# Residual block with per-image mixed 3x3 kernels: two whole-image passes move to GpSimd, conv1 groups are evacuated whole, and the prologue and the order of steps are rewritten

## What is computed

```python
xn = (x - mean_c) / sqrt(var_c + 1e-5)                    # per image and channel
gate = softmax(mean_pixels(xn) @ gate_w.T + gate_b)       # 7 experts
kw1 = sum_e gate[e] * experts_w1[e] + conv1_w             # 32x32x3x3, likewise kb1, kw2, kb2
out1 = relu(conv3x3(xn, kw1) + kb1)
out  = x + (xn + conv3x3(out1, kw2) + kb2)
```

## Time and profile before

| what | value |
|---|---|
| time, median of 3 runs | 386.82 us |
| the 3 runs | 386.42, 389.31, 386.82 us |
| span of the profiled execution | 389.2 us |
| time nearest to that span | 389.31 us |
| mean granted TensorE clock | 0.940 of full speed |
| busy PE, DVE, ACT, POOL | 326.8, 308.1, 300.3, 44.5 us |
| DMA, share of 16 engines' span | 69.7% |

### The profile page before, as it was taken

One profiled execution on the slowest core, in us unless ns is written; L12 is line 12 of the kernel. 1 busy time (PEld: TensorE's weight loads), 2 busy tenths in 40 slices (PEclk: granted clock), 3 DMA queues, 4 the chain that ended last, 5 costly groups with the idle time before them and its releaser, 6 DMA issues.

```text
span 389.2 us, 8418 instructions
## 1 busy us (share of the span) xinstructions
PE 326.8 (84%) x2983; PEld 198.4 (51%) x2983; DVE 308.1 (79%) x709; ACT 300.3 (77%) x373; POOL 44.5 (11%) x80
## 2 busy tenths in 40 slices
PE   3218698996999699996979979996999979999984
PEld 2117345654555355653535555653656545655663
DVE  4899978988689886998688797898689897777432
ACT  2357499986897968977897868978789768976950
POOL 7262302010100101010000101010010101000000
PEclk9556999998999989998999989999999989999998
DMA  7949915495948959396856949497885956092354
GB/s 169 224 95 196 205 30 125 107 203 137 202 92 187 182 142 220 86 210 148 178 127 149 223 111 203 96 196 147 188 167 123 217 128 147 22 207 53 92 123 121
DMA packets 107146, 58.19 MB, mean 149 GB/s; under 512 B 102496, under 2 KB 103008, under 8 KB 107104
## 3 DMA queue, kind: packets, MB, share of 16 engines
q1 hardware_dynamic: 106912, 57.62, 69.7%
q0 software_dynamic: 192, 0.01, 0.1%
HBM read 19.47 MB, written 18.87 MB: 99 GB/s over the span
## 4 chain that ended last, share of the span: by engine, by line
DVE 39%; PE 22%; issue 15%; ACT 13%; DMA 6%; SPq 3%; DVEq 1%; ACTq 0%
PE pg L393 20%; DVE mix L677 11%; DVE a L706 6%; DVE stats L621 6%; DVE img L718 5%; DMA c<-a 5%; ACT c L558 4%; ACT a L544 4%; ACT hid L544 2%; DVE a L668 2%; DVE wts L696 2%; DVE wts L699 2%; SPq L282 1%; DVE gate L661 1%; PE pg L357 1%
## 5 line engine op out<-in xcount | busy, mean ns | idle before, releaser
L393 PE MATMUL pg<-a,wts 128*64 128x480 f16 (+1 forms) x1440 | 303.5, 368 | 24.8 <-DVE img L718 18.2
L393 PE MATMUL pg<-c,wts 128*64 128x480 f16 (+1 forms) x1440 | 308.3, 372 | 6.1 <-ACT a L544 3.2
L393 PEld LDWEIGHTS pg<-c,wts 128*64 128x64 f16 x1440 | 156.1, 111 | 81.7 <-issue 6.8
L393 PEld LDWEIGHTS pg<-a,wts 128*64 128x64 f16 x1440 | 156.1, 112 | 64.5 <-issue 14.6
L544 ACT ACTIVATE hid<-pg,col 128x480 f32<-128x480 f32 (+3 forms) x112 | 58.9, 541 | 47.6 <-PE pg L393 25.6
L558 ACT COPY c<-a 64x2352 f32<-64x2352 f32 x32 | 68.7, 2148 | 0.2
L677 DVE SCALAR_TENSOR_TENSOR mix<-bank,gate,mix 128x386 f32<-128x386 f32 x96 | 63.9, 665 | 2.3
L706 DVE TENSOR_TENSOR a<-hid,a 128x480 f16<-128x480 f32 (+3 forms) x112 | 54.9, 512 | 12.2 <-ACT a L544 11.6
L544 ACT ACTIVATE a<-pg,col 128x480 f16<-128x480 f32 (+3 forms) x112 | 59.2, 544 | 0.4
L718 DVE SCALAR_TENSOR_TENSOR img<-pg,img 128x480 f32<-128x480 f32 (+1 forms) x80 | 48.1, 631 | 11.2 <-PE pg L393 9.9
L621 DVE BATCH_NORM_STATS2 stats<-img 128x6 f32<-128x384 f32 x96 | 45.5, 541 | 0.0
(11 more groups left out here) (60 smaller groups left out, 133.8 us busy)
## 6 DMA issues: line engine op xcount, KB each, us to landing
c<-a SPq DMA_DIRECT2D x28, 588.0 KB, 9.0
img<-in_x SPq DMA_DIRECT2D x56, 288.0 KB, 5.3
out<-img SPq DMA_DIRECT2D x60, 180.0 KB, 2.9
out<-img SPq DMA_DIRECT2D x60, 108.0 KB, 1.9
c<-a SPq DMA_DIRECT2D x8, 294.0 KB, 4.4
img<-in_x SPq DMA_DIRECT2D x16, 144.0 KB, 4.4
out<-img SPq DMA_DIRECT2D x4, 120.0 KB, 2.1
out<-img SPq DMA_DIRECT2D x8, 60.0 KB, 1.7
```

The lines of the kernel that those rows point to most:

```text
L393: last = nc.tensor.matmul(pg[g][side * 64:side * 64 + 64, at:at + nb * W].rearrange("p (b w) -> p b w", w=W), wts[s.c % WSETS][kind][:, v, ...
```

## The change

GpSimd takes the image's low part for every image, in four pieces, and the residual, in two. It also computes the pooled mean from the statistics (so `normalise` no longer sums) and its product with the gate weights. `hidden` and `hidden_low` do each group in one piece; a new step `clear_rim` on VectorE sets the two bands outside the image to zero afterwards. The factor 16 of the weights is applied where the kernels are copied, and `scale_shared` goes. The kernel loads are issued by ScalarE instead of SP, the kernels of conv1 first. In the prologue conv1 of image 0 runs in two passes over all five groups, first the products that need the high part only. ScalarE does `normalise` and `high_part` of image s+2 in slot s, not s+1, and residual is gone from its queue.

```diff
+PARTS = 4
 # TensorE
 def warm_up():
+    pe.wait_ge(whi_ok, 1)
 ...
+def first_conv1():
+    s = Sample(0, 0)
+    pe.wait_ge(w_ok, 1)
+    pe.wait_ge(crossed1_high[0], 32)
+    pe.wait_ge(wt_act, 4)
+    pe.wait_ge(wt_dve, 4)
+    for g in range(GRP):
+        products(0, s, g, PRODUCTS[:2], *conv1_sides(s, g))
+    for g in range(GRP):
+        products(0, s, g, PRODUCTS[2:], *conv1_sides(s, g)).then_inc(conv1_ps, 1)
 ...
+    warm_up()
+    first_conv1()
+    conv1_group(Sample(0, 1), 0)
+    gather_rows(Sample(0, 2))
+    conv1_group(Sample(0, 1), 1)
+    conv1_group(Sample(0, 1), 2)
+    conv1_group(Sample(0, 1), 3)
+    logits(Sample(0, 2))
     def slot(s):    # TensorE
-        ... conv1 0, 1, 2, logits(s+1), conv1 3, gather_rows(s+2), conv1 4, conv2(s-1) 0..4
+        ... conv1 0, 1, 2, 3, gather_rows(s+2), conv1 4, conv2(s-1) 0, 1, logits(s+2), conv2(s-1) 2, 3, 4
 # ScalarE
-def residual(t): ...
 def hidden(s, g):
     ...
-    pieces = group_pieces(g)
+    j0, j1 = g * SPG, (g + 1) * SPG
+    for o in (hid[g_parity(s, g)][:, :, :], a2[s.parity][:, HI, j0:j1, 1:1 + W]):
+        last = nc.scalar.activation(o, pg[g][:, 0:SPG * W]..., ACT.Relu, bias=c[:, B1:B1 + 1], scale=HS / WS)
+    load_kernels()
+    for n in range(0, 8, 2):
+        copy_kernels(n)
+    ...
+    high_rows(Sample(0, 0), 0, NB // 2)
+    exponentials(Sample(0, 0))
+    high_rows(Sample(0, 0), NB // 2, NB).then_inc(hi1_ok, 1)
+    normalise(Sample(0, 0))
+    weights_high(Sample(0, 0))
+    exponentials(Sample(0, 1))
+    high_part(Sample(0, 1))
+    normalise(Sample(0, 1))
+    weights_high(Sample(0, 1))
     def slot(s):    # ScalarE
+        hidden(s) 0, 1, 2, 3, normalise(s+2), hidden(s) 4, weights_high(s+1), high_part(s+2),
+        cross2(s), exponentials(s+2)
 # VectorE
-def pooled_times_gate(t): ...
-def low_part(t): ...
+def clear_rim(s, g):
+    dve.wait_ge(lo2_ok, s.number * GRP + g + 1)
+    p0, j = (P - 2 * C, 0) if g == 0 else (P - C, NS - 1)
+    nc.vector.memset(a2[s.parity][p0:p0 + C, :, j, 1:1 + W], 0.0).then_inc(rim_ok, 1)
     def slot(s):    # VectorE
+        finish(s-2) 4, statistics(s+2), hidden_low(s) 0, aggregate(s+2), clear_rim(s) 0,
+        softmax_out(s+1), mixture(s+1) 0, hidden_low(s) 1, channel_moments(s+2),
+        mixture(s+1) 1, 2, 3, hidden_low(s) 2, mixture(s+1) 4, 5, 6, hidden_low(s) 3,
+        biases(s+1), weights(s+1), hidden_low(s) 4, clear_rim(s) 4,
+        finish(s-1) 0, 1, softmax_in(s+2), finish(s-1) 2, 3
 # GpSimd
 def coefficients(t):
     ...
+    link(nc.gpsimd.tensor_tensor(c[:, SCALED:SCALED + 1], mv[t.ring][:, 0:1], c[:, RSTD:RSTD + 1], ALU.mult))
+    link(nc.gpsimd.tensor_tensor(c[:, POOLED:POOLED + 1], c[:, SCALED:SCALED + 1], c[:, NBIAS:NBIAS + 1], ALU.add))
+    nc.gpsimd.tensor_tensor(gwp[t.ring][:, :], table[:, 0:E], c[:, POOLED:POOLED + 1].to_broadcast([P, E]),
+                            ALU.mult).then_inc(gwp_ok, 1)
+def low_part(t, q0, q1):
+    for q in range(q0, q1):
+        b0, b1 = q * NB // PARTS, (q + 1) * NB // PARTS
+        if q == 0:
+            pool.wait_ge(hi1_ok, t.number + 1)
+            pool.wait_ge(xh_ok, t.number + 1)
+        last = nc.gpsimd.tensor_tensor(a1[t.parity][:, LO, b0:b1, 1:1 + W], xh[t.parity][:, b0:b1, :],
+                                       a1[t.parity][:, HI, b0:b1, 1:1 + W], ALU.subtract)
+    ...
+def residual(t):
+    c = col[t.ring]
+    for b0, b1 in ((0, NB // 2), (NB // 2, NB)):
+        last = nc.gpsimd.tensor_scalar(img[t.ring][:, b0:b1, :], img[t.ring][:, b0:b1, :],
+                                       c[:, RS1:RS1 + 1], c[:, RB:RB + 1], ALU.mult, ALU.add)
+    last.then_inc(res_ok, 1)
     def slot(s):    # GpSimd
-        run(coefficients, s, 2, 2)
+        run(residual_bias, s, 0, 0)
+        run(low_part, s, 1, 2, 0, PARTS)
+        run(coefficients, s, 2, 2)
+        run(residual, s, 0, 0)
```

More of the change, by code:

```diff
@@ L603, in _ @@
-            schedule(slot, act, -1, 3, 16)
+            def slot(s):
+                run(hidden, s, 0, 0, 0)
+                run(hidden, s, 0, 0, 1)
+                run(hidden, s, 0, 0, 2)
+                run(hidden, s, 0, 0, 3)
+                run(normalise, s, 2, 2)
+                run(hidden, s, 0, 0, 4)
+                run(weights_high, s, 1, 2)
+                run(high_part, s, 2, 2)
+                run(cross2, s, 0, 0, 0)
+                run(cross2, s, 0, 0, 1)
+                run(exponentials, s, 2, 2)
@@ L797, in _ @@
+            biases(Sample(0, 1))
+            weights(Sample(0, 1))
             statistics(Sample(0, 2))
-            mixture(Sample(0, 1), 3)
-            mixture(Sample(0, 1), 4)
             aggregate(Sample(0, 2))
             hidden_low(Sample(0, 0), 0)
-            mixture(Sample(0, 1), 5)
-            mixture(Sample(0, 1), 6)
+            channel_moments(Sample(0, 2))
+            clear_rim(Sample(0, 0), 0)
             hidden_low(Sample(0, 0), 1)
-            channel_moments(Sample(0, 2))
@@ L806, in _ @@
-            biases(Sample(0, 1))
             hidden_low(Sample(0, 0), 2)
-            weights(Sample(0, 1))
             hidden_low(Sample(0, 0), 3)
-            pooled_times_gate(Sample(0, 2))
             hidden_low(Sample(0, 0), 4)
+            clear_rim(Sample(0, 0), GRP - 1)
             statistics(Sample(0, 3))
-            hidden_low(Sample(0, 1), 0)
-            aggregate(Sample(0, 3))
             softmax_in(Sample(0, 2))
-            low_part(Sample(0, 2))
-            softmax_out(Sample(0, 2))
@@ L866, in _ @@
-            schedule(slot, dve, -2, 2, 17, link, 7)
+                run(hidden_low, s, 0, 0, 0)
+                run(aggregate, s, 2, 2)
+                run(clear_rim, s, 0, 0, 0)
+                run(softmax_out, s, 1, 1)
+                run(mixture, s, 1, 1, 0)
+                run(hidden_low, s, 0, 0, 1)
+                run(channel_moments, s, 2, 2)
+                run(mixture, s, 1, 1, 1)
+                run(mixture, s, 1, 1, 2)
+                run(mixture, s, 1, 1, 3)
+                run(hidden_low, s, 0, 0, 2)
@@ new lines, in slot @@
+                run(mixture, s, 1, 1, 4)
+                run(mixture, s, 1, 1, 5)
+                run(mixture, s, 1, 1, 6)
+                run(hidden_low, s, 0, 0, 3)
+                run(biases, s, 1, 1)
+                run(weights, s, 1, 1)
+                run(hidden_low, s, 0, 0, 4)
+                run(clear_rim, s, 0, 0, GRP - 1)
+                run(finish, s, -1, 0, 0)
+                run(finish, s, -1, 0, 1)
+                run(softmax_in, s, 2, 2)
+                run(finish, s, -1, 0, 2)
@@ L869, in _ @@
+                run(finish, s, -1, 0, 3)
+            schedule(slot, dve, 1, 2, 17, link, 7)
         @block.gpsimd
```

310 lines of the change are left out of this document (99 added, 211 removed).

## The result

The changed kernel takes **373.6 us** in the median (370.98 to 374.03, four runs) against 387.2 for the kernel before on the same chip: ratio 0.961, 95% interval 0.956 to 0.966. The profiled execution has a span of 371.8 us.

What follows compares the result with a forecast made beforehand. VectorE was taken to set the pace at 22.2 us a slot, falling to 16.7 + 0.6 + 2 x 1.3 = 19.9. Slots gain 12 x 2.3 = 28 us, the fill gives back 8: 367 us, range 354 to 409.

Steps and rivals of the forecast that it cites:

- my sum: Steady slot: VectorE's 16.7 us, plus 0.6 for the low part, plus 2 x 1.3 for the residual: 19.9 against 22.2.
- VectorE's slot: VectorE's own work in a steady slot falls from 19.2 to 16.7 us; waits for GpSimd come on top.
- the first quarter: Low part on GpSimd: its first of four pieces meets hidden_low 4, charged 0.6 us a slot, ends 0 and 3.7.
- VectorE loses both pieces: Residual on GpSimd runs beside mixtures, hidden_low and weights without cover; VectorE waits out both pieces, 2 x 1.3 us a slot.
- The price of a piece: One residual piece of 1152 columns on GpSimd, the open number: taken as 1.3 us, upper end 3.3.
- the slow rival: Residual pieces of 2.3 to 3.3 us hold up the mixtures; kernel slower, 391 to 419 us; chance 0.28.
- PE's floor: PE's work in a steady slot: 18.9 us added up, 19.2 with some slack for gaps.
- the PE-bound rival: Cheap or covered residual brings VectorE under 19.2 us a slot, so PE sets the pace: 352 to 360 us; chance 0.17.
- Transfers bound: no chance.: DMA needs 17.0 of 19.9 us a slot, 85%; cross1 is released half a slot early; no chance of its own.
- The fill: Prologue gets longer: conv2(0) starts at 66.3 against 59.78, slot 2 at 79.4; 8 us given back.
- The end: finish(12,0) at 315.5, 49.4 us to the last finish, 4.6 for stores: span 369.5, off the median 367 us.
- The parts: Slots: small GpSimd operations cost 0, finish and statistics keep their lengths, VectorE's waits for L517 (1.10 us) and L508 go.

Runs made afterwards that it cites:

- the repeat: The changed kernel itself, unedited, timed again on the chip of other follow-up runs: 373.3 us, ratio 0.962 to the kernel before.
- experiment 1: The changed kernel with SP issuing the copy cross1(s) ahead of load(s+2) from image 1 on: 360.7 us, ratio 0.925.
- Experiment 9: The kernel of experiment 1 with the loop going round once (LAPS 1 for 2), later slots written out: 356.8 us, ratio 0.917.
- experiment 10: The kernel before the change, with only SP's order turned round, cross1(s) ahead of load(s+2): 387.1 us, ratio 0.996.
- experiment 11: The changed kernel with hidden and hidden_low doing groups 0 and 4 in pieces again, clear_rim out: 378.5 us, ratio 0.974.
- 12: The changed kernel with conv1 of image 0 written group by group in place of two passes: 374.3 us, ratio 0.961.
- experiment 5: The changed kernel with the residual back on ScalarE in one pass, the low part left on GpSimd: 368.7 us, ratio 0.947.

## Why the prediction was right, and where it was right by luck

The time, 367 against 373.6, and the side are right. The slot average of 19.9 us came out at 19.92 in one execution and 20.20 in the repeat, but not by my sum: it is the mean of slots of 18.7 to 18.9 us and of others made long by a late copy or the loop. That it hit was luck.

- **VectorE's slot.** I had 16.7 of its own, 0.6 for the first quarter and 2.6 for both residual pieces. Measured is 18.0 us busy in a slot, 1.7 of it lost to the residual (0.84 in the mixtures, 0.89 in `weights`), so 16.3 of its own. A loss of 1.1 at `hidden_low`(s,4) comes in two slots only (1.74 for 0.65, at 79.17 and 198.34). VectorE alone would have allowed 18.0 to 19.1, not 19.9. The overcharge is in "VectorE loses both pieces": GpSimd waits for VectorE as well. Two pieces of 1.30 last 3.77 us there, and part of VectorE's work gets done in the 1.2 us more.
- **The price of a piece.** The line's own view (duration in ns, shortest/median/longest of 32) has 1.30 us as the shortest, as predicted. The prediction's prices per column, 2.74 and 1.0 ns, have the 0.16 us fixed of the two-input row taken off first, which it doesn't say; 1.30 us is 0.99 ns so counted. L908's 2.74 did not carry over to this shape, and the slow rival, 0.28, which stood on it, was wrong. What a piece lasts above 1.30 it has a VectorE instruction of two inputs beside it:

```profile
L872 POOL TENSOR_SCALAR img<-img,col x32: 1297/1703/2090, 56.3 to 336.0; 128x1152 f32<-128x1152 f32 x32
```

- **PE's floor.** I added up 18.9 us and put 19.2 with slack; experiments 1 and 9 show 18.85. Experiment 9's 356.8 us lies inside the PE-bound rival's 352 to 360.
- **"Transfers bound: no chance."** This step failed. The 17.0 of 19.9 us was a sound bound on bytes, and `cross1` is indeed released early: at 165.0 for a copy that PE wants at 181.2. But I reasoned from the release and from the bytes and left out what lies between, the copy's place in SP's queue (7.0 to 8.0 us into the slot) and its time to landing beside a load (8.6 to 10.8 us). It could have been read from the kernel before. There the copy landed 19.5 us or more into every slot, and in the four slots of 20.8 us PE had been ready at 17.3. The gap that ends at 270.8, to which I gave no cause, ended 0.25 us after a copy had landed; which of copy and `finish` held it the rows do not separate. The order cost 6.8 us in the slots and 4.7 in the fill (experiment 1). The loop's jump back, about 4 us, I did not have at all. It seems to lie in the kernel before too (in experiment 10 the slot at that place lasts 25.2 us among ones of 21 to 22), but no experiment took it out there.
- **The fill.** The end of mixture 1 was predicted for 42.3 and that of its cast for 42.8; the cast starts at 42.72. `weights`(1), which conv1(1) needs, I had at 44.5, and it ended at 44.6. But conv1(1) waited for its copy, issued behind load(3), until 49.24, and came back at half the clock; these PE rows and windows answer to the earlier trace rows:

```profile
49.24 0.50 PE L375 MATMUL pg<-a,wts 128*64 128x384 f16 x1 [5.25 <-DMA c<-a]
...
68.83 0.60 PE L358 MATMUL pstat<-triples,same 128*128 128x12 f32 x2 [9.51 <-DVE triples L607]
```

```profile
44.00:49.00 5.00, 0.00 (x0) 0.00 (x0) 4.67 (x12) 1.58 (x4) 0.00 (x0) 0.71 1.03 227
49.00:53.00 4.00, 3.76 (x19) 2.06 (x19) 0.00 (x0) 1.09 (x2) 0.00 (x0) 0.51 1.27 213
53.00:58.00 5.00, 5.00 (x49) 2.92 (x50) 2.62 (x8) 2.96 (x3) 3.68 (x7) 1.00 0.44 73
```

In the window from 49 PE does 19 matmuls in 4 us at a clock of 0.51, the 1.2 GHz level; from 53 it does 49 in 5. The gathering for image 3, predicted for 64.1, is at 68.83, conv2(0) at 73.0 for 66.3, and slot 2 at 84.3 for 79.4.
- **The end.** `finish`(12,0) is at 320.2 for 315.5, 4.7 late as the fill is, and from it to the last `finish` are 47.1 us for 49.4. So the span is 371.8 for 369.5. Of the 6.6 us between 367 and 373.6 this is 2.3. The rest is the step from span to median, which I took as 2.4 down and which came out 1.8 up. In every profiled execution from the kernel after on, the time is 1.8 to 1.9 us above its own span; the span of 389.2 was thus, by estimate, that of an execution of about 391, and not of the 389.31 that stands nearest to it.
- **The parts.** Small operations on GpSimd delayed nothing, `finish` and the statistics keep their lengths, and the waits of the earlier trace rows for L517 and L508 are gone, all as predicted. Costed at next to nothing, and wrong: the pieces (5 us, experiment 11). The two passes, which I did not cost, are worth nothing (12).

Why experiment 5 is faster than the change, with SP's order the same, is seen in the rows, though no run isolates it. By its view PE's waits for the copy fall from 9.2 to 1.8 us, and with all waits that end at a landing from 12.4 to 5.2. The copy lands as late in VectorE's slot as ever (17.4 to 19.2 us), but in the two slots where PE waits for it, it was ready only after 18.4 us in place of 17.5: a VectorE that is shorter by 1.7 us follows PE more closely, and its `finish` releases the stores, the load and the copy behind them earlier, seen from PE.

## What to carry to other kernels

When a change shortens a slot, redo the arrival of every transfer that a matmul waits for: what its queue issues ahead of it, plus its time to landing, against the new time of need. That the data are ready early says little; here they were 16 us early and the copy was late. A transfer that the next matmul needs should not stand behind one that is needed later. A wait that a view puts down to one engine may have ended with a landing: look for what landed just before. An average slot that fits a forecast says little; print the slots one by one, since here 18.8 and 21 us made a predicted 19.9. Judge a part (the residual on GpSimd, the order on SP) only together with the bound it works under: each of these changed its sign or its size when the other changed.

## What the runs showed of the hardware

- An exclusive wait between VectorE and GpSimd is decided by hundredths of a microsecond: 4.91 or 0.66 us for the same instruction, and it is decided anew at each instruction: in four pieces the same low part held `hidden_low` for 1.1 us at most.
- The copy inside SBUF, two transfers of 588 KB each, had a median of 8.7 us from issue to landing behind the load of 1.15 MB, and of 6.8 us ahead of it.
- A loop of two rounds cost 3 to 4 us more than one round and the rest written out (360.7 and 356.8 us, ratios 0.925 and 0.917), with the same work.
